# Cross-attention and a feed-forward layer on one core: VectorE's order in the loop, and the preparation reordered

## The reference

```
x = x + xattn(layernorm(x), ctx)     # 8 heads of 64; q = x Wq, k = ctx Wk, v = ctx Wv
                                     # softmax(q k^T / 8) v, then Wo and bo
n = layernorm(x)
h = layernorm(n) * gamma + beta
y = silu(h @ w1 + b1)                # w1 = (q1 - 128) * s1, 256 x 1024; w2 = (q2 - 128) * s2, 1024 x 256
x = x + n + 0.5 * (y @ w2 + b2)
```

## Time and profile before

| | |
|---|---|
| time, median of 3 runs | 201.87 us (201.49 to 201.95) |
| profiled execution, its own time | 201.96 us |
| its span, first to last instruction | 200.2 us |
| TensorE busy | 187.3 us, 94% |
| VectorE, ScalarE, GpSimd busy | 61%, 61%, 55% |
| granted TensorE clock | 1.00 of full speed |

### The profile page before, as it was taken

The page is one execution under the profiler, slowest core; times in us unless marked ns, Lnnn a source line. Parts: engine busy times, 40 slices in busy tenths (PEclk is TensorE's granted clock), DMA queues, the critical chain, the costliest instruction groups (busy, mean ns, idle before and its releaser), DMA issues.

```text
span 200.2 us, 3855 instructions
## 1 busy us (share of the span) xinstructions
PE 187.3 (94%) x1502; PEld 180.1 (90%) x1502; DVE 122.9 (61%) x262; ACT 121.9 (61%) x227; POOL 109.6 (55%) x135
## 2 busy tenths in 40 slices
PE   6989879789889999999999999999999998998994
PEld 6979669689878999899989999999999998998894
DVE  0487985899859544954495558746683577532341
ACT  2267960499708981787268934894289626754480
POOL 5034993269951957096708861695249544367020
DMA  6999950000000000000000000000000000000101
GB/s 164 318 403 368 260 166 5 2 0 3 0 27 1 29 0 0 29 26 0 3 26 26 3 0 28 29 2 0 26 29 0 3 0 28 28 0 3 49 3 52
DMA packets 9480, 10.72 MB, mean 54 GB/s; under 512 B 2268, under 2 KB 8183, under 8 KB 9335
## 3 DMA queue, kind: packets, MB, share of 16 engines
q1 hardware_dynamic: 8837, 9.70, 14.8%
q10 hardware_dynamic: 626, 0.79, 1.4%
HBM read 8.38 MB, written 2.10 MB: 52 GB/s over the span
## 4 chain that ended last, share of the span: by engine, by line
PE 51%; POOL 18%; DVE 12%; SPq 12%; issue 3%; DMA 1%; ACT 1%; DVEq 0%; ACTq 0%
PE H L785 18%; PE T L773 13%; PE T L797 10%; POOL y_lo L280 5%; SPq L213 4%; SPq L207 4%; PE S L752 4%; PE S L759 3%; POOL x_sb L274 3%; POOL rstd L262 3%; PE S L706 2%; DVE probs L524 2%; DVE smax L522 2%; POOL res_scale L266 2%; DMA vw_lo<-bo_lo 1%
## 5 line engine op out<-in xcount | busy, mean ns | idle before, releaser
L252 POOL TENSOR_TENSOR probs<-probs,rsum 128x616 f32<-128x616 f32 x16 | 19.1, 1217 | 39.9 <-DVE rsum L533 39.9
L280 POOL TENSOR_TENSOR y_lo<-y,y_hi 128x512 fp32r<-128x512 f32 x28 | 37.8, 1362 | 4.9 <-ACT y_hi L394 4.3
L785 PE MATMUL H<-hT_hi,w_hi 128*128 128x256 f32 x128 | 36.8, 288 | 2.2 <-issue 1.8
L797 PE MATMUL T<-w_hi,y_hi 128*128 128x256 f32 x128 | 37.0, 289 | 1.1 <-POOL y_lo L280 0.5
L363 ACT ACTIVATE probs<-probs,rstd 128x616 f32<-128x616 f32 x16 | 12.9, 808 | 40.4 <-DVE probs L524 40.4
L797 PE MATMUL T<-w_hi,y_lo 128*128 128x256 f32 x128 | 35.7, 279 | 0.0
L797 PE MATMUL T<-w_lo,y_hi 128*128 128x256 f32 x128 | 35.7, 279 | 0.0
L785 PE MATMUL H<-hT_hi,w_lo 128*128 128x256 f32 x128 | 35.5, 278 | 0.0
L785 PE MATMUL H<-hT_lo,w_hi 128*128 128x256 f32 x128 | 35.5, 277 | 0.0
L390 ACT ACTIVATE y<-H,vec 128x256 f32<-128x256 f32 x64 | 26.6, 468 | 8.4 <-PE H L785 8.4
L785 PEld LDWEIGHTS H<-hT_hi,w_hi 128*128 128x128 f32 x128 | 24.0, 188 | 3.8 <-issue 2.2
(11 more groups left out here) (115 smaller groups left out, 442.8 us busy)
## 6 DMA issues: line engine op xcount, KB each, us to landing
q_sb<-in_L_ffn_fc_q SPq DMA_DIRECT2D x2, 1024.0 KB, 13.2
out_x<-x_sb SPq DMA_DIRECT2D x16, 128.0 KB, 1.7
x_sb<-in_x SPq DMA_DIRECT2D x7, 256.0 KB, 5.6
s_sb<-in_L_ffn_fc_scales SPq DMA_DIRECT2D x2, 512.0 KB, 11.8
s_sb<-in_L_ffn_fc_scales SPq DMA_DIRECT2D x1, 1024.0 KB, 17.7
wq_sb<-in_L_xattn_Wq SPq DMA_DIRECT2D x1, 512.0 KB, 6.0
wo_sb<-in_L_xattn_Wo SPq DMA_DIRECT2D x1, 512.0 KB, 8.6
wk_sb<-in_L_xattn_Wk ACTq DMA_DIRECT2D x1, 384.0 KB, 4.5
```

What stands on the lines that cost most here:

```text
L252: nc.gpsimd.tensor_tensor(p, p, rsum[:, j, :].unsqueeze(2).to_broadcast([P, HEADS, J]), ALU.mult).then_inc(norm_done, 1)
L280: nc.gpsimd.tensor_tensor(y_lo[:, two, :], y[:, two, :], f32(y_hi[:, two, :]), ALU.subtract).then_inc(y_lo_done, 1)
L785: ins = mm(r[:, q * W:(q + 1) * W], wt[:, c, m * P:(m + 1) * P], ht[:, c, :], start=i == 0, stop=i == len(steps) - 1)
L797: ins = mm(o, yt[:, m, j * P:(j + 1) * P], wt[:, m, :], start=m == 0 and i == 0, stop=m == M - 1 and i == 2)
```

## The change

Four things are altered.

1. SP: the first batch's bias rows are issued ahead of q2, s2 and the last five loads of x; gamma, beta and b1 ahead of them; the second batch's bias rows stay behind the loads.
2. The start: VectorE sums Wq ahead of stats1(0) and makes x_lo(0) after place_v; ScalarE makes wqT ahead of x_hi(0).
3. hn: GpSimd makes rstd2 a tile at a time, the residual's part apart and last (9 instructions instead of 6 for a pair), and make_hn waits for one tile's value. In the first pair VectorE makes hn between the maxima and the subtraction of S1.0, ScalarE does scale_h(0) ahead of exponential(1, 0), and TensorE transposes hn ahead of both remaining VW products, into H0 instead of S0.
4. The loop: finish_tile(a-2, 0) moves from behind make_hn(a-1), that is ahead of the maxima of pass a, to behind both subtractions and ahead of split_h(a-1). TensorE does three matmuls of fc2 instead of six ahead of the transposes of hn.

```diff
-             ... ("S1.0", "S0"), ("S1.1", "S1"), ("VW1.1", "T0"), ("HT0", "S0"), ("VW1.2", "T1")]
+             ... ("S1.0", "S0"), ("S1.1", "S1"), ("HT0", "H0"), ("VW1.1", "T0"), ("VW1.2", "T1")]
@@ SP
                 sp.dma_start(x_sb[:, pair(2), :], ...)
-                sp.dma_start(q2_sb[:, :, :], ...)
-                sp.dma_start(s2_sb[:, :, :], ...)
                 ... gamma, beta, b1
+                sp.wait_ge(bo_split, 1)
+                wait_freed(sp, "VW0.2")
+                sp.dma_start(f32(vw_hi[BIAS_ROW:BIAS_ROW + 1, JC - 1, :]), f32(bo_hi[:, :])).then_inc(bias_rows[0], 16)
+                sp.dma_start(f32(vw_lo[BIAS_ROW:BIAS_ROW + 1, JC - 1, :]), f32(bo_lo[:, :])).then_inc(bias_rows[0], 16)
+                sp.dma_start(q2_sb[:, :, :], ...)
+                sp.dma_start(s2_sb[:, :, :], ...)
                 for a in range(3, NA):
                     sp.dma_start(x_sb[:, pair(a), :], ...)
-                ... both batches' bias rows
+                wait_freed(sp, "VW1.2")
+                ... the second batch's bias rows
@@ GpSimd, rsqrt2(a)
-                    pool.wait_ge(mv2_done, a * UT + UT)
+                    for j in range(UT):
+                        pool.wait_ge(mv2_done, a * UT + j + 1)
+                        nc.gpsimd.tensor_scalar(vars2[:, o, 1, j:j + 1], mv2[:, o, j, 1:2], 1.0 + EPS, EPS * EPS,
+                                                ALU.mult, ALU.add).then_inc(vars2_done, 1)
+                        pool.wait_ge(vars2_done, a * 3 + j + 1)
+                        nc.gpsimd.tensor_tensor(rstd2[:, o, 1, j:j + 1], vars2[:, o, 1, j:j + 1], neg_half[:, 0:1],
+                                                ALU.pow).then_inc(rstd2_done, 1)
                     nc.gpsimd.tensor_scalar(vars2[:, o, 0, :], mv2[:, o, :, 1], EPS, None, ALU.add).then_inc(vars2_done, 1)
-                    nc.gpsimd.tensor_scalar(vars2[:, o, 1, :], ...)
-                    pool.wait_ge(vars2_done, a * 2 + 2)
-                    nc.gpsimd.tensor_tensor(flat(rstd2[:, o, :, :]), flat(vars2[:, o, :, :]), neg_half[:, 0:2 * UT],
-                                            ALU.pow).then_inc(rstd2_done, 1)
+                    pool.wait_ge(vars2_done, a * 3 + 3)
+                    nc.gpsimd.tensor_tensor(rstd2[:, o, 0, :], vars2[:, o, 0, :], neg_half[:, 0:UT], ALU.pow).then_inc(res_rstd_done, 1)
@@ ScalarE
-                x_hi(0)
                 center_wq(0)
                 center_wq(1)
+                x_hi(0)
...
-                exponential(1, 0)
                 act.wait_ge(vec_in, 16 * 2)
                 scale_h(0)
+                exponential(1, 0)
@@ VectorE
-                stats1(0)
                 sum_wq(0)
                 sum_wq(1)
-                x_lo(0)
+                stats1(0)
                 dve.wait_ge(vT_zeroed, 1)
                 place_v(0)
                 place_v(1)
+                x_lo(0)
...
-                shift_scores(1, 0)
+                score_maxima(1, 0)
                 make_hn(0)
+                subtract_maxima(1, 0)
                 shift_scores(1, 1)
...
-                finish_tile(0, 0)
                 for a in range(2, NA):
                     shift_scores(a, 0)
                     shift_scores(a, 1)
+                    if a < LAST:
+                        finish_tile(a - 2, 0)
                     split_h(a - 1)
...
                     make_hn(a)
-                    if a < LAST - 1:
-                        finish_tile(a - 1, 0)
@@ TensorE
                 scores(1, 1)
+                h_transposes(0)
                 make_vw(1, 1)
-                h_transposes(0)
                 make_vw(1, 2)
...
-                    fc2(a - 2, 1, range(2))
+                    fc2(a - 2, 1, range(1))
                     h_transposes(a - 1)
-                    fc2(a - 2, 1, range(2, M))
+                    fc2(a - 2, 1, range(1, M))
```

More of the change, by code:

```diff
@@ L177, in build_program @@
         neg_rstd_done, shift_done, hn_done = sem("neg_rstd_done"), sem("shift_done"), sem("hn_done")
+        res_rstd_done = sem("res_rstd_done")
         h_done, h_hi_done, res_part, res_done = sem("h_done"), sem("h_hi_done"), sem("res_part"), sem("res_done")
@@ L211, in _ @@
                     sp.dma_start(b1_sb, b1.rearrange("(n p) -> p n", p=P)).then_inc(vec_in, 16)
+                sp.wait_ge(bo_split, 1)
+                wait_freed(sp, "VW0.2")
+                sp.dma_start(f32(vw_hi[BIAS_ROW:BIAS_ROW + 1, JC - 1, :]), f32(bo_hi[:, :])).then_inc(bias_rows[0], 16)
+                sp.dma_start(f32(vw_lo[BIAS_ROW:BIAS_ROW + 1, JC - 1, :]), f32(bo_lo[:, :])).then_inc(bias_rows[0], 16)
+                sp.dma_start(q2_sb[:, :, :], q2.rearrange("(n p) f -> p n f", p=P)).then_inc(q2_in, 16)
+                sp.dma_start(s2_sb[:, :, :], s2.rearrange("(o m) e -> o m e", o=1).to_broadcast([P, M, D])).then_inc(s2_in, 16)
                 for a in range(3, NA):
                     sp.dma_start(x_sb[:, pair(a), :], x_v[:, pair(a), :]).then_inc(x_in[a], 16)
[L216 to L221, removed]
+                wait_freed(sp, "VW1.2")
+                sp.dma_start(f32(vw_hi[BIAS_ROW:BIAS_ROW + 1, 2 * JC - 1, :]), f32(bo_hi[:, :])).then_inc(bias_rows[1], 16)
+                sp.dma_start(f32(vw_lo[BIAS_ROW:BIAS_ROW + 1, 2 * JC - 1, :]), f32(bo_lo[:, :])).then_inc(bias_rows[1], 16)
                 for f in range(NA):
@@ L256, in rsqrt2 @@
                     o = a % 2
-                    pool.wait_ge(mv2_done, a * UT + UT)
-                    nc.gpsimd.tensor_scalar(vars2[:, o, 0, :], mv2[:, o, :, 1], EPS, None, ALU.add).then_inc(vars2_done, 1)
-                    nc.gpsimd.tensor_scalar(vars2[:, o, 1, :], mv2[:, o, :, 1], 1.0 + EPS, EPS * EPS,
-                                            ALU.mult, ALU.add).then_inc(vars2_done, 1)
-                    pool.wait_ge(vars2_done, a * 2 + 2)
-                    nc.gpsimd.tensor_tensor(flat(rstd2[:, o, :, :]), flat(vars2[:, o, :, :]), neg_half[:, 0:2 * UT],
-                                            ALU.pow).then_inc(rstd2_done, 1)
-                    pool.wait_ge(rstd2_done, a + 1)
+                    for j in range(UT):
[5 more added lines that the diff above has]
+                                                ALU.pow).then_inc(rstd2_done, 1)
+                    nc.gpsimd.tensor_scalar(vars2[:, o, 0, :], mv2[:, o, :, 1], EPS, None, ALU.add).then_inc(vars2_done, 1)
+                    pool.wait_ge(vars2_done, a * 3 + 3)
+                    nc.gpsimd.tensor_tensor(rstd2[:, o, 0, :], vars2[:, o, 0, :], neg_half[:, 0:UT], ALU.pow).then_inc(res_rstd_done, 1)
+                    pool.wait_ge(res_rstd_done, a + 1)
                     nc.gpsimd.tensor_scalar(res_scale[:, o, :], rstd2[:, o, 0, :], 1.0, None, ALU.add).then_inc(shift_done, 1)
@@ L516, in x_lo, with score_maxima, subtract_maxima, shift_scores @@
                     nc.vector.tensor_tensor(flat(xT_lo[:, :, :]), ps[bank][:, 0:C * W], flat(f32(xT_hi[:, :, :])), ALU.subtract).then_inc(freed[bank], 1)
-                def shift_scores(a, j):
+                def score_maxima(a, j):
                     name = f"S{a}.{j}"
                     s = wait_filled(dve, name)[:, :].rearrange("p (n c) -> p n c", n=2)[:, :, 0:HALF].rearrange("p n (h j) -> p n h j", j=J)
+                    nc.vector.tensor_reduce(smax[:, j, :].rearrange("p (n h) -> p n h", n=2), s, AX_X, ALU.max).then_inc(max_done, 1)
+                def subtract_maxima(a, j):
+                    bank = place[f"S{a}.{j}"][0]
+                    s = ps[bank][:, :].rearrange("p (n c) -> p n c", n=2)[:, :, 0:HALF].rearrange("p n (h j) -> p n h j", j=J)
                     mx = smax[:, j, :].rearrange("p (n h) -> p n h", n=2)
-                    nc.vector.tensor_reduce(mx, s, AX_X, ALU.max).then_inc(max_done, 1)
                     dve.wait_ge(max_done, a * UT + j + 1)
                     nc.vector.tensor_tensor(probs[:, j, 0:HJ].rearrange("p (n h j) -> p n h j", n=2, j=J), s,
-                                            mx.unsqueeze(3).to_broadcast([P, 2, HEADS // 2, J]),
-                                            ALU.subtract).then_inc(freed[place[name][0]], 1)
+                                            mx.unsqueeze(3).to_broadcast([P, 2, HEADS // 2, J]), ALU.subtract).then_inc(freed[bank], 1)
+                def shift_scores(a, j):
+                    score_maxima(a, j)
+                    subtract_maxima(a, j)
                 def invert_sums(a, j):
@@ L550, in make_hn @@
                 def make_hn(a):
-                    dve.wait_ge(rstd2_done, a + 1)
                     for j in range(UT):
                         t, o = a * UT + j, a % 2
+                        dve.wait_ge(rstd2_done, t + 1)
                         nc.vector.scalar_tensor_tensor(hn[:, j, :], x_sb[:, t, :], mv2[:, o, j, 0:1],
```

2 lines of the change are left out of this document (removed), and 2 rows, old and new, of the table order.

## The result

The change takes 197.55 us (median of 4 runs, 197.44 to 197.65) where the kernel before, run beside it, takes 201.91 (4 runs, 201.49 to 202.46). The ratio is 0.9781, with a 95% interval of 0.9765 to 0.9797: 2.2% faster. The forecast was 197.4.

The account below looks back on a forecast made before the run. TensorE, busy 94% of the span, bounds the kernel, so only its waits can be won. -1.49 - 0.23 - 0.72 - 2.34 + 0.33 = -4.45 from 201.96 gives 197.5, as median 197.4 us; range 196.1 to 199.0.

Parts of the forecast that it names:

- Part 1: Bias rows: issued earlier on SP, so TensorE's wait ahead of attention_out(0, 0) goes whole, -1.49 us.
- two bounds for the landing: Second bias copy lands at about 19.5 (2.9 us after issue) or, taking b1's 10.0 us, at 26.4.
- Part 2: Start: with Wq's sums ahead of x_lo on VectorE, V1's bank is empty 0.23 us earlier, -0.23 us.
- Part 3: First pair: hn right behind the maxima and earlier transposes let fc1(0, 0) start at 38.10, -0.72 us.
- Part 4: Loop: finish_tile behind the maxima shortens five stretches from scores' end to fc1 to 3.41 us each, -2.34 us.
- VectorE decides by 0.28: In the loop's stretches VectorE's chain still exceeds TensorE's own 3.13 us of work by 0.28 us.
- the first two rivals: Loop gives back little, 198.5 us (chance 0.20); TensorE alone decides in the loop, 196.0 us (chance 0.12).
- Part 5: GpSimd's rstd tile by tile: hidden in the loop, lengthens the chain in the last pair, +0.33 us.
- The other rivals: Bias copies land too late, 198.9 us (0.05); GpSimd's small operations at their price beside VectorE, 202.8 us (0.04).

Follow-up runs that it names:

- experiment 2: The kernel before with only SP's new order (first batch's bias rows ahead of q2, s2 and later x loads): 200.65 us, ratio 0.994.
- experiment 4: The changed kernel with x_hi(0), stats1(0) and x_lo(0) put back in their old places at the start: 197.81 us, ratio 0.9801.
- experiment 8: The kernel of experiment 5 with the last two parts of lower_y moved from GpSimd to VectorE, behind make_hn(7): 194.19 us, ratio 0.9624.
- experiment 7: The changed kernel with the first pair's old order on VectorE, ScalarE and TensorE, hn's transposes again into S0: 197.89 us, ratio 0.9815.
- Experiment 6: The changed kernel with the old rsqrt2 and make_hn, rstd of both tiles again in one power: 197.87 us, ratio 0.9808.
- experiment 3: The kernel before with only finish_tile(a-2, 0) moved and hn's transposes three fc2 matmuls earlier, rstd2 still joint: 199.46 us, ratio 0.9889.
- experiment 5: The changed kernel with finish_tile(a-2, 0) moved further back, behind split_h and both inverse sums: 195.66 us, ratio 0.9695.
- experiment 1: The changed kernel run again without any edit: 197.64 us, ratio 0.979.

## Why the prediction was right

**Part 1 (forecast -1.49).** Right: -1.57 in the trace of the change and of experiment 2, -1.23 in the latter's medians. Of its two bounds for the landing the lower nearly held: 2.5 us from issue for 2.9, at 19.9 for 19.5, since the issue came later. b1, whose 4-byte descriptors stand ahead of the copies, landed at 19.5, the first copy with it and the second 0.4 later, so this trace tells neither for nor against the order in the ring that the Trainium skill states (DMA: Bandwidth & Descriptors, "Queues, rings and completion order").

**Part 2 (-0.23).** Right in size, hidden in the trace of the change: experiment 4 shows 0.18 from V to scores(0, 0), and experiment 8 beside before 0.21, with V1's buffer empty at 12.83 where the forecast had 12.84. Yet the first transposes of probabilities come 0.40 later in the trace of the change than before, where the forecast had them 0.23 earlier. Here the forecast's sum lacked a term: Wk's projection starts at 6.19 us instead of 5.77, and V waits for Wv's load. The start scatters in that way whatever the kernel (below).

**Part 3 (-0.72).** The size is right: 4.38 to 3.64, -0.74, by experiment 7. The step that failed is the ascription: the part says "both tiles' rstd are there" and takes that as given, but only the rsqrt2 of part 5 makes it so. Experiment 6 puts 0.43 of the 0.74 on it. fc1(0, 0) was forecast at 38.10 and came at 38.61: 0.63 late from the start (0.40 later instead of 0.23 earlier), less 0.08 by which part 1 gained more and 0.04 by which this part did.

**Part 4 (-2.34).** Right: -2.42 in experiment 3's medians, and stretches of 3.38 to 3.39 for a forecast of 3.38, taken as 3.41. The sum maxima to fc1 plus finish_tile was exact to 0.01 us, and "VectorE decides by 0.28" is what experiment 5 measured. With it the first two rivals fall: the loop gives the whole gain, and TensorE alone decides only once finish_tile is gone from the stretch, at 3.10 for the forecast's 3.13. The waits ahead of fc1 for hT_lo, forecast as 0.1 to 0.3, are not listed in the view of waits for the loop (the 0.3 in it is the last pair's, which before has too); by the length of the stretch, 3.38 against 3.10, they are 0.28 each.

**Part 5 (+0.33).** The cost is 0.26 in the chain on GpSimd, and that it is near the forecast is in part luck. A power of one column takes 0.55 us for the 0.57 forecast. But from the first vars of tile 1 to res_scale the chain takes 2.45 us (172.91 to 175.36), not 2.01, and from there to y_lo 0.64 instead of before's 1.14. The forecast's sum priced the small operations as if hn did not touch them. hn(0) lies on the second tile's vars (0.33 us for the 0.19 of the first pair) and hn(1) on the residual's (0.52 for 0.22), 0.44 together; before, the two hn lay on res_scale and its neighbour (0.51 and 0.43, for 0.22 and 0.23 in the first pair), 0.49 together. The held operations end 0.05 to 0.09 us behind hn, so the price is what is left of hn: 0.28 of its 0.45 us at 172.91, which is why hn(0) cost 0.14 and not up to 0.45. The Trainium skill (SBUF — State Buffer, "Who interferes with whom") calls the port pair that VectorE and GpSimd share an exclusive lock; the trace agrees. What the part missed is its use: with the 0.43 in the first pair it is worth about -0.17 in the traces, not +0.33. That holds only beside part 3: with the old order the first pair's stretch is 4.38 with the new rsqrt2 (experiment 7) as with the old (before).

**The other rivals.** q2 and s2 were not waited for, so the bias wait was not replaced. GpSimd's powers kept their prices (0.55, 0.71) and only operations beside hn grew, so nothing held finish_tile for a=2: add_b2 ended at 57.67, and it was wanted at 58.2.

The total agrees within 0.15 us, which is better than its terms deserve: +0.40 up to the first transposes of probabilities, where the forecast had -0.23, and -0.40 behind the last ones, where it had nothing, cancel in this pair of traces. Experiments 2 and 3 give -1.23 and -2.42, 3.65 together; the whole is -4.24 in experiment 1. That leaves 0.6 for parts 2, 3 and 5, which forecast 0.62 together.

## What to carry to other kernels

When an instruction that waits for a third engine stands ahead of work that the bounding engine needs, moving it behind that work can be worth the whole wait, as it was here, and the new limit is the plain sum of the instructions between: add it up, compare it with the bounding engine's own work in the stretch, and if it still exceeds that, move the instruction once more (here 1.4 us more by the stretches, 2.0 by the medians). A value made for a chain tile by tile pays only where its consumer stands ready for the first tile: look at each place separately, since the same edit gained 0.43 us in one and cost 0.26 in the other. A short wait of TensorE can cost more than the profile draws, as here, so read it from start to start.

## What the runs showed of the hardware

**Two waits of TensorE cost more than they were drawn.** 0.81 us drawn in two waits cost 1.34 to 1.37 (experiment 8). A matmul of fc2 is drawn 0.28 us long, while the next starts 0.11 to 0.12 behind it when nothing waits, so each drawn wait leaves out the difference, about 0.16; and the matmul behind the waiting one came 0.1 late as well.

**A small operation of GpSimd ended just behind the hn that it met.** Over the ten traces 116 of its small operations started 0.03 to 0.17 us into an hn of VectorE. Whatever they take alone (0.19 to 0.24 us), 112 of them ended 0.05 to 0.09 behind that hn's end; the other four, at 0.03 to 0.04, took their 0.22. A power that was already running when hn began kept its price: 0.55 us at 72.05 in the change, with hn from 72.25. So did one that started 0.02 behind hn: 0.72 at 34.06. The 1.55 us of the power in the earlier trace rows fits in: in the change it runs from 43.60 to 45.15, and the preparation of w2 on VectorE ends at 44.57, 0.58 earlier.

**The start scatters.** Wk's projection starts between 5.77 and 6.33 us in the ten traces, without a relation to what was changed: 5.77 in before, 5.78 in experiment 8, 6.19 in the change, 5.86 in its repetition. Of TensorE's first instructions, the same in both, experiment 8 and the change have in the same two microseconds:

```profile
4.00:6.00 2.00, 1.83 (x15) 1.54 (x14) 0.47 (x1) 0.00 (x0) 0.00 (x0) 1.00 1.04 318
```
```profile
4.00:6.00 2.00, 2.00 (x13) 1.57 (x11) 0.43 (x1) 0.00 (x0) 0.00 (x0) 1.00 1.05 281
```

15 matmuls against 13, at the same granted clock, with loads coming in at 318 and 281 GB/s; in the change the load of Wv then came too late for V: 0.2 us are drawn, 0.36 are lost from start to start. What slows the start in some executions was not tested.

**The last section has two lengths.** From the last fc1 to the last matmul, 96 matmuls without a wait take 11.57 us in the traces of before, of experiment 1 and of experiment 3, and 11.16 or 11.17 in the other seven. Experiments 1 and 5, in which these instructions are the same:

```profile
181.87:193.44 11.57, 11.57 (x96) 11.36 (x96) 3.47 (x6) 6.55 (x14) 1.31 (x1) 1.00 0.04 13
```
```profile
180.16:191.33 11.17, 11.16 (x96) 10.96 (x96) 3.47 (x6) 6.54 (x14) 1.30 (x1) 1.00 0.04 13
```

The matmuls start 0.119 us apart on average in one and 0.115 in the other, at a granted clock of 1.00 in both; the change shows both lengths in two executions. A difference of 0.4 us between two single traces of this kernel therefore means nothing by itself. The cause stays open.
